# Grouped-query attention on one core: the output projection done one head a slot, from rounded high and low parts

## Time and profile before

| what | value |
|---|---|
| median of 3 runs | 1946.65 us (1946.47 to 1948.49) |
| the profiled execution | 1946.17 us |
| its span in the profile | 1944.3 us |
| PE busy over the span | 1562.1 us (80%) |
| DVE busy | 1295.5 us (67%) |
| ACT busy | 932.3 us (48%) |
| POOL busy | 715.9 us (37%) |

### The profile page before, as it was taken

The page is one execution under the profiler, slowest core; times in us unless marked ns, Lnnn a source line. Parts: engine busy times, 40 slices in busy tenths (PEclk is TensorE's granted clock), DMA queues, the critical chain, the costliest instruction groups (busy, mean ns, idle before and its releaser), DMA issues. The chain is left out here.

```text
span 1944.3 us, 28391 instructions
## 1 busy us (share of the span) xinstructions
PE 1562.1 (80%) x9276; PEld 1214.6 (62%) x9286; DVE 1295.5 (67%) x2160; ACT 932.3 (48%) x2281; POOL 715.9 (37%) x735
## 2 busy tenths in 40 slices
PE   6899789878974655292769999999999999997372
PEld 4444568666851223281758888888888888885372
DVE  3665364766467998644647777777777778775743
ACT  2365335233524331251546666666666666663341
POOL 3011243324367764644832222222222222220743
PEclk9899799889987887595889999999999999999586
DMA  3320323222310001364000000000000000000443
GB/s 75 53 50 2 96 84 109 66 87 87 106 48 0 0 0 56 117 128 141 11 1 12 12 12 2 22 1 23 1 23 1 22 1 12 1 1 19 152 108 107
DMA packets 62059, 90.04 MB, mean 46 GB/s; under 512 B 10192, under 2 KB 44240, under 8 KB 61920
## 3 DMA queue, kind: packets, MB, share of 16 engines
q1 hardware_dynamic: 53664, 65.68, 11.4%
q0 software_dynamic: 8256, 22.56, 5.1%
HBM read 62.38 MB, written 19.40 MB: 42 GB/s over the span
## 5 line engine op out<-in xcount | busy, mean ns | idle before, releaser
L1294 DVE TENSOR_REDUCE gqa_neg_max<-acc 128x1 f32<-128x1024 f32 (+7 forms) x256 | 193.1, 754 | 173.2 <-PE acc L1403 172.1
L1180 ACT ACTIVATE gqa_probsT_high<-aux 128x512 fp32r<-128x512 f32 x288 | 172.0, 597 | 249.5 <-PE aux L1411 248.6
L1299 DVE TENSOR_TENSOR gqa_probsT_low<-aux,gqa_probsT_high 128x512 fp32r<-128x512 f32 x288 | 197.8, 687 | 29.8 <-ACT gqa_probsT_high L1180 25.6
L1189 ACT ACTIVATE gqa_probs<-acc,gqa_neg_max 128x1024 f32<-128x1024 f32 (+7 forms) x256 | 189.3, 739 | 29.6 <-DVE gqa_neg_max L1294 24.6
L1411 PE MATMUL aux<-ident,gqa_probs 128*128 128x128 f32 x1152 | 174.4, 274 | 0.0
L1087 POOL TENSOR_SCALAR gqa_q_scale<-gqa_q_scale 128x4 f32<-128x4 f32 x64 | 16.3, 255 | 381.0 <-ACT gqa_square L1124 380.7
L1422 PE MATMUL aux<-gqa_probsT_high,gqa_v_high 128*128 128x512 f32 x288 | 146.7, 509 | 1.0 <-DVE gqa_probsT_low L1299 1.0
L472 POOL DMA_INDIRECT f_xs<-tokens,f_slot_token x108 | 104.4, 967 | 108.4 <-PE aux L752 44.3
L1091 POOL TENSOR_TENSOR gqa_ln_xn<-gqa_ln_xn 128x512 f32<-128x512 f32 x64 | 82.2, 1285 | 147.0 <-DVE gqa_ln_xn L1219 146.9
L1434 PE MATMUL aux<-gqa_wo,gqa_oT 128*128 128x256 f32 x512 | 132.4, 381 | 4.4 <-DVE stream L1287 3.5
L1401 PE MATMUL acc<-gqa_k_low,gqa_q_high 128*128 128x512 f32 (+5 forms) x384 | 132.1, 344 | 0.0
(11 more groups left out here) (411 smaller groups left out, 4444.9 us busy)
## 6 DMA issues: line engine op xcount, KB each, us to landing
f_w<-in_f_up SPq DMA_DIRECT2D x64, 256.0 KB, 3.2
outputs_by_slot<-f_y_tile SPq DMA_DIRECT2D x108, 128.0 KB, 2.5
f_w<-in_f_down SPq DMA_DIRECT2D x64, 128.0 KB, 3.6
mat_qk<-mat_high SPq DMA_DIRECT2D x64, 64.0 KB, 2.3
tokens<-f_ln_xn SPq DMA_DIRECT2D x4, 1024.0 KB, 4.6
gqa_w_q<-in_g_wq SPq DMA_DIRECT2D x8, 512.0 KB, 3.6
gqa_wo<-in_g_wo SPq DMA_DIRECT2D x8, 512.0 KB, 3.8
mat_qk<-mat_low SPq DMA_DIRECT2D x32, 64.0 KB, 2.3
```

Source lines behind the costliest of these rows:

```text
L1180: act.activation(probsT_high[:, u % RING, :], aux[:, u % 2, :], ACT.Copy).then_inc(cell_high_ready, 1)
L1189: act.activation(out, scores(n), ACT.Exp, bias=neg_max[:, j % (2 * JOBS):j % (2 * JOBS) + 1], accum_out=row_sum[:, n // 2 % 4, m, n % 2:n ...
L1294: dve.tensor_reduce(neg_max[:, j % (2 * JOBS):j % (2 * JOBS) + 1], scores(n), AXY, ALU.max, negate=True).then_inc(max_ready, 1)
L1299: dve.tensor_tensor(probsT_low[:, u % RING, :], aux[:, u % 2, :], probsT_high[:, u % RING, :].bitcast(F32), ALU.subtract).then_inc(cell_lo ...
```

The core of the diff:

```diff
-        RING = 4
-        w_q = sb("w_q", [P, DC * QUAD * HD])
+        RING = 3
+        w_raw = sb("w_raw", [P, DC * QUAD * HD])
-        wo = sb("wo", [P, 2, QUAD, D])
+        wo_high = sb("wo_high", [P, QUAD, D], F32R)
+        wo_low = sb("wo_low", [P, QUAD, D], F32R)
+        oT_high = sb("oT_high", [P, 2, QUAD * P], F32R)
+        oT_low = sb("oT_low", [P, 2, QUAD * P], F32R)
...
-            at = {"project": {0: 2 * band + 3, 6: 2 * band + 4}, "turn": {2: 2 * band + 2, 4: 2 * band + 3}}[kind]
+            at = {"project": {1: 2 * band + 3, 7: 2 * band + 4}, "turn": {3: 2 * band + 2, 5: 2 * band + 3}}[kind]
...
+        def out_head(z):
+            n, m = (2 * band - 4, 3) if c == 0 else (2 * band - 3, c - 2) if 2 <= c < 6 else (2 * band - 2, c - 6)
+            return (n, m) if 0 <= n < TILES and 0 <= m < QUAD else None
...
+            def outputs(n):
+                pool.wait_ge(oT_copied, n + 1)
+                if n >= 2:
+                    pool.wait_ge(wo_done, QUAD * (n - 1))
+                pool.tensor_copy(oT_high[:, n % 2, :], oT[:, n % 2, :]).then_inc(oT_high_ready, 1)
+                pool.wait_ge(oT_high_ready, n + 1)
+                pool.tensor_tensor(oT_low[:, n % 2, :], oT[:, n % 2, :], oT_high[:, n % 2, :].bitcast(F32),
+                                   ALU.subtract).then_inc(oT_low_ready, 1)
+            for z in range(SLOTS):
+                for n in ended(z):
+                    outputs(n)
+                n = query_tile(z - 1, "project")
+                if n is not None:
+                    queries(n)
...
             for z in range(SLOTS + 1):
+                add(z - 1)
                 if z < SLOTS and job(z):
                     ...
-                add(z - 1, 0)
                 ...
-                add(z - 1, 1)
...
+            def project_out(n, m):
+                pe.wait_ge(oT_low_ready, n + 1)
+                pe.wait_ge(wo_low_ready, 2 * (n // NT) + m // 2 + 1)
+                if QUAD * n + m >= 1:
+                    pe.wait_ge(added, QUAD * n + m)
+                rows = slice(m * P, (m + 1) * P)
+                for c, (a, b) in enumerate(three(oT_high[:, n % 2, rows], oT_low[:, n % 2, rows], wo_high[:, m, :], wo_low[:, m, :])):
+                    last = pe.matmul(wo_bank[:, m % 2 * D:(m % 2 + 1) * D], a, b, start=c == 0, stop=c == 2)
                 last.then_inc(wo_done, 1)
...
-                if out_pair(z):
-                    project_out(*out_pair(z))
                 if 1 <= u <= CELLS * BANDS:
                     weigh(u - 1)
+                if out_head(z):
+                    project_out(*out_head(z))
```

More of the change, by code:

```diff
@@ L1020, in new_quad, with wo_part @@
             return band // 4 + 1 if c == at and band % 4 == 2 and band // 4 + 1 < QUADS else None
+        def wo_part(z):
+            band, c = divmod(z, CELLS)
+            return (band // 4, {4: 0, 6: 1}[c]) if c in (4, 6) and band % 4 == 1 and band // 4 < QUADS else None
         block = ctx.enter_context(nc.Block())
@@ L1103, in _ @@
             keys(3)
-            for n in range(3, TILES):
-                queries(n)
+            def outputs(n):
[12 more added lines that the diff above has]
+                    queries(n)
         @block.scalar
@@ L1199, in _ @@
                     split_q(quad)
+                if wo_part(z):
+                    quad, half = wo_part(z)
+                    act.wait_ge(wo_in, 16 * quad + 16)
+                    if quad >= 1:
+                        act.wait_ge(wo_done, QUAD * NT * quad - 2 + 2 * half)
+                    act.activation(wo_high[:, 2 * half:2 * half + 2, :], wo[:, 2 * half:2 * half + 2, :], ACT.Copy).then_inc(wo_high_ready, 1)
         @block.vector
@@ L1317, in _ @@
                     split_q(quad)
+                if wo_part(z):
+                    quad, half = wo_part(z)
+                    dve.wait_ge(wo_high_ready, 2 * quad + half + 1)
+                    dve.tensor_tensor(wo_low[:, 2 * half:2 * half + 2, :], wo[:, 2 * half:2 * half + 2, :],
+                                      wo_high[:, 2 * half:2 * half + 2, :].bitcast(F32), ALU.subtract).then_inc(wo_low_ready, 1)
         @block.tensor
```

73 lines of the change are left out of this document (30 added, 43 removed).

## The result

The changed kernel takes 1949.59 us (median of 20 runs, 1945.95 to 1952.17). The kernel before, run beside it, took 1945.10 (20 runs, 1940.18 to 1948.49). The ratio is 1.0027, 95% interval 1.0019 to 1.0034: slower, by about 4.5 us. I had forecast slower by 14. The profiled execution took 1950.95 us with a span of 1949.2; before it was 1946.17 with 1944.3.

A forecast was written before the change was run, and what follows sets the result against it. PE, busy 98.92 of 100, bounds the loop: waits up 5.2 us, work down 2.7, so four bands 2.5 us longer. Seven fours add 17.5, ends return 3, on 1946.2: 1960.7, with the median 1961 us; range 1944 to 1974.

The forecast's parts named there:

- `w_q_low`: One band in four: its 1.80 us on DVE ahead of slot 3's additions delays a head and slot 4's weighing by 1.15 us.
- The bound, and the saving: PE bounds the attention loop; heads at 0.35 us each in rounded parts save 0.68 us a band, 2.7 in four.
- The chain in slot 0: PE's head waits for DVE's addition behind the rotary products, 3.76 us after slot 8's turn; 3.5 us lost in four bands.
- The copies `oT`: ACT's copy stands behind squares or the queries' high part, so a tile's first weighing waits: 0.8 and 0.4, together 1.2 us.
- `turn_queries`: PE still waits for DVE's rotary products two slots after the partner's projection: 1.3 us in four bands where 1.9 was.
- A rule beside it: DVE instructions with two SBUF inputs and POOL's SBUF reads exclude each other; POOL's added work can delay only wo_low and w_q_low.
- The sum: Waits of four bands rise from 2.0 to 7.2 us, work falls 2.7, four bands grow 2.5; whole kernel 1961 us.
- The ends: The loop's first and last bands give back 3 us of the 17.5 us added over seven fours of bands.
- (a): Rival: the new wait for the addition does not arise, 22 to 35 us gained, 1912 to 1925 us; chance 0.12.
- (b): Rival: the waits are half of those counted, equal to the saving, 1943 to 1951 us, no change; chance 0.12.
- (c): Rival: same waits and POOL late too, 1 to 2 us more in four bands, 1966 to 1978; chance 0.16 with (d).
- (d): Rival: a head on PE costs more than 0.35 us; at 0.45, 13 us more, 1974; chance 0.16 with (c).

The follow-up runs named there:

- one_f32_head: Changed kernel with each head as one plain f32 matmul instead of three float32r ones, all else kept: 1958.91 us, four bands 102.23.
- pairs_in_parts: Kernel before with the projection in rounded parts, still two heads at a time, two slots later, old query places and addition order: 1933.63 us, ratio 0.9938.
- rope_after_add: Changed kernel with even tiles' three rotary products moved on DVE from the end of slot 8 to behind slot 0's addition: 1932.38 us, ratio 0.9926.
- one_product_less: Changed kernel with one of the three rotary products left out for even tiles from the fifth on: 1939.53 us in one run, four bands 99.75.
- weights_slots45: Changed kernel with w_q_high moved to ACT's slot 4 and w_q_low to DVE's slot 5: 1945.25 us, ratio 1.0007.
- rope_after_add_low3: Changed kernel with even tiles' rotary products behind slot 0's addition, and w_q_low in slot 3 instead of slot 2: 1935.14 us, ratio 0.9946.
- low_weights_slot4: Kernel before with w_q_low made in DVE's slot 4 instead of slot 2: 1944.61 us, ratio 0.9992.

## Why the prediction was right in direction and wrong in size

Two steps of the prediction failed. It took the 1.80 us of `w_q_low` as the length of the instruction, and so a wait of 1.15 us in four bands that measured 0.45; and it let everything outside the loop, and the distance from the profiled execution to the median, stand as before. The wait that makes the change a loss was right.

**The bound, and the saving: right.** A head costs 0.35 us from start to start, as counted, and the three matmuls start 0.12 apart. one_f32_head shows that the saving is real (0.08 a head), and pairs_in_parts shows it where the additions do not hold it: 1.5 us less in four bands and 12 us in all, after a longer wait for the rotary products has taken some of it back.

**The chain in slot 0: right.** 3.83 us against 3.76 from turn to head in the band shown. The waits there are 0.76, 0.76, 0.96 and 0.35, with 0.14 at one weighing: 3.0; and each costs 0.09 more because the first matmul behind a wait is longer (0.36 instead of 0.28 in the rows above), so 3.3 in all against 3.5. rope_after_add and one_product_less show the cause. I wrote that these waits would be 0.4 to 0.9 and 25 us in all; they are 0.35 to 0.96, and some 24 in all (8 times 3.0).

**The copies `oT`: right.** 0.78 and 0.37 us, where I took 0.8 and 0.4.

**`turn_queries`: right in size, in part by luck.** 0.61 + 0.48 and 0.14 in small pieces, 1.2 against 1.3. But for the largest of them I named only the rotary products. With `w_q_high` and `w_q_low` moved it is 0.32 us (weights_slots45), and moving `w_q_low` alone does not shorten this wait (rope_after_add_low3): so 0.29 of the 0.61 come from ACT's `w_q_high`, which I had not counted.

**`w_q_low`: the term that failed.** I took its 1.80 us from the earlier trace rows as its own length and counted 1.15 us for the head and the weighing behind it. It measured 0.36, with the longer first matmul 0.45. The instruction is 1.21 us long, and POOL, not DVE, pays for the overlap in its new place; by the rows that is 0.59 of the 0.70 too much. No run made it 1.80 long in this place, so the size of its share is worked out and not measured, and the last 0.1 has no named cause. The paragraph "A rule beside it" had the rule right and used it in one direction only: it asked what POOL's new work would add to 1.80, and not whether 1.80 already held POOL's old work. The row that would have told it was in the trace of before: POOL's L1095 lies under each of the seven `w_q_low` of the loop, in the same way.

**The sum.** The waits of four bands are 3.3 + 1.2 + 0.45 + 1.2 = 6.2, not 7.2. By the forecast's own sum, 6.2 - 2.0 - 2.7, four bands should then grow by 1.5 instead of 2.5; they grew by 1.67. (Of the 0.2 between them about 0.1 is my rounding: the old waits are 1.9 in the prediction's own first paragraph.) Over seven fours that is 5.8 us less. The ends gave 3.2 back (7 times 1.67 is 11.7; the loop from first score to last addition grew by 8.5, from 811.6 to 820.1), against 3 forecast. From the first score to the tenth turn the changed kernel gained 3.3 us on the one before, and over the last 27 turns another 3.7, where the waits of 0.76 are gone; but from the last turn to the last addition it lost 3.7. There the first head waits 2.35 us for POOL's `oT_low`, and the heads start 1.34, 1.65 and 1.65 us apart, not 1.2. The row of 1794 to 1800 us goes with the longer steps: the granted clock is 0.52 there, near the lower of its two levels (1.2 GHz), where it was 1.00 from 1790 to 1794, and from a head's start to its addition's it is 1.02 us instead of 0.71. The remaining 3.7 us of the difference lie outside the loop. From the span's start to the first score it was 1.0 us shorter, and from the last addition to the end 2.6 us shorter (149.3 against 151.9). The first is no effect of the change: the first score lies anywhere from 976.1 to 980.7 us in the thirteen profiles, and at 978.2 in low_weights_slot4, whose code up to there is that of the kernel before. The second also holds in the other profiles: 151.9 and 153.1 us in the two kernels with the old projection, 149.0 to 150.7 in the eleven with the projection in its new places. 1.1 us of it is the start of the next layer: its first statistics on DVE begin 4.2 us behind the end of the last addition before, and 3.1 us behind it now. Why the rest is shorter was not tried; kernels with the same code there differ by up to 1.7. 14.5 - 5.8 - 0.2 - 3.7 = 4.8, which is 1950.95 - 1946.17. Last, I put the median 0.5 us above the profiled execution, from three runs of the kernel before; over 20 runs the median lies 1.36 below it (and 1.07 below it for the kernel before). That is another 1.9 us of the distance from 1961 to 1949.59.

**The rivals.** (a), the wait not arising, is out. (b), half of the waits, is what the time looks like, but not how it came: three of the four kinds of wait stood at their full size. (c) is out as a cost of four bands, since no wait of PE in the middle of the loop has POOL as releaser; one at the loop's end has (2.35 us). (d) is out at 0.35 a head.

## What to carry to other kernels

When an operation that frees a buffer is put first in a queue's next turn, price everything at the end of the turn before, for that is now ahead of it; here 1.3 us of rotary products, moved behind it, turned a loss of 0.3% into a gain of 0.7%. Before a duration is used as the length of an instruction, look at what the other engines did meanwhile: with two engines that exclude each other the same instruction was 1.21 or 1.80 us, and its neighbour 0.61 or 1.60. And a wait named after one engine may come from the engine behind that one; moving the suspect costs one run and can clear it.
